# Values of a gated delta attention: four tap matmuls, or one projection convolved by GpSimd

## The chip, the cores and the metric

The kernel runs on one core of a Trainium2 chip. The core has a matrix engine (TensorE, PE), three engines for elementwise work (VectorE or DVE, ScalarE or ACT, GpSimd or POOL) and a queue that issues transfers (SyncE, SP). The metric is the device time of one launch in microseconds; lower is better. Every engine works through its own queue in order, and the queues meet at semaphores. GpSimd works on SBUF; matmul results lie in PSUM banks until VectorE or ScalarE takes them out.

## The reference

The program is four transformer layers with different attentions and feed-forward parts. The change is in the attention of the second layer, a gated delta rule over 4 sequences, run here on 1024 tokens each, with 8 heads of 128:

```python
mixed = einsum('bth,ch->btc', hidden_states, qkv_w)
mixed = causal_depthwise_conv(mixed, conv_w)      # 4 taps for each channel
z = einsum('bth,vh->btv', hidden_states, z_w)
q, k, v = split(mixed, 3)                         # 8 heads of 128 each
beta = sigmoid(bb); alpha = exp(-exp(A_log) * softplus(aa + dt_bias))
def step(S, inp):
    q_t, k_t, v_t, beta_t, alpha_t = inp
    S = S * alpha_t
    kv = einsum('bhk,bhkv->bhv', k_t, S)
    S = S + einsum('bhk,bhv->bhkv', k_t, (v_t - kv) * beta_t)
    return S, einsum('bhk,bhkv->bhv', q_t, S)
o = o * rsqrt(mean(o * o) + EPS) * norm_w * (z * sigmoid(z))
out = einsum('btv,hv->bth', o, out_w)
```

## The kernel before

The kernel solves the recurrence in chunks of 128 tokens. A chunk is one head and one block of 128 tokens in all four sequences at once, so most tiles are 128 x 4 x 128, written 128x512 in the profile. There are 8 heads x 8 blocks = 64 chunks (`CHUNKS`). The stage `a1s`, written by `delta_chunk_steps`, is one loop of 67 turns; every turn works on four chunks at different ages, which `phases(step)` names: `j` (the newest: keys and queries are projected and convolved, decay factors are made), `q` (the triangular system of the chunk is inverted), `r` (the state `S` is applied and updated), `e` (the output leaves). In the change "order" means the order of statements in this loop: each engine's queue is written out by hand.

What matters in a turn:

- The gram matrix of the keys (`gram_ps`, in `bank0`) times `Estrict` gives `N`; its diagonal blocks `Nc` are copied by ACT and masked by POOL into `lev`.
- The inverse is grown in six rounds. Round n: PE `zt(n)` (32 small matmul records from `lev` and `T`, L1035), ACT copies `Zt` (L1239), PE `tx(n)`, DVE `grow(n)` adds to `XTc` and transposes it into `T` (L1385, L1387). Round n+1 needs that `T`. Rounds 5 and 6 join blocks of 32 and of 64 in `XT`. PE puts other matmuls between `zt` and `tx` and between rounds.
- DVE's `place()` (L1391) copies four diagonal blocks of `XTc` into `XT` after round 4.
- Keys and queries are projected by one matmul each (L1143, L1161), copied into `hist` by ACT, and convolved by DVE: one tensor_scalar (L1371) and three scalar_tensor_tensor steps (L1373) for each of the two. These are the "conv" steps.
- The values are projected and convolved at once by PE. `xs` holds the chunk's normalized tokens with three tokens of history (copied by POOL, L1316, L1318), and the weights are held four times, scaled by each tap (ACT, L1215, once a head). `vtok_part(b)` adds up four matmuls of shifted tokens (L1109); ACT copies the result into `vtok`, which has tokens on the partitions.
- DVE multiplies `o` by the gate into `y` and, at the end of the turn, by the reciprocal of its root mean square (L1471); PE turns `y`, ACT copies `yT`, PE projects it out.
- POOL makes `newS`, `lev` (L1328, L1329), `sb` (L1335), `Estrict` (L1342) and `Eincl` (L1345).

The queue of PE for one turn is, in order: gram(q), kS(r), yT(e), qS(r), ktok(q), K raw(j), out(e), u(r), zt1, Q raw(j), tx1, o(r), zt2, S(r), tx2, dt(j), zt3, value part 0, tx3, part 1, zt4, part 2, tx4, part 3, zt5, qk(q), tx5, z(q), zt6, tx6. `Chain` is a helper that makes an engine wait for its own last instruction.

## Time and profile before

| | us |
|---|---|
| median of three runs | 8394.17 |
| lowest and highest | 8381.44 and 8395.7 |
| the profiled execution | 8398.92 |
| its span, first to last instruction | 8397.2 |

| engine | busy us in the span | share |
|---|---|---|
| PE | 7016.8 | 84% |
| DVE | 5867.6 | 70% |
| ACT | 4051.7 | 48% |
| POOL | 2918.4 | 35% |

The stage `a1s` runs from about 1041 to 2607 us of the span. "PE" rows are matmuls, "PEld" rows are weight loads, which overlap them. One float32 matmul leaves two records, so four matmuls read "x8". In a timeline row the first number is the start, the second the time from the first start to the last end of the merged instructions, and brackets hold the idle time of that engine before the row and what ended it. Group rows hold the count, then busy us and the mean ns of one, then idle time.

### The profile page before, as it was taken

How to read it: one execution, taken by the hardware profiler on the slowest of the kernel's cores; microseconds unless marked ns; L12 is line 12 of the kernel's file. 1: busy time of each engine (PE TensorE's matmuls, PEld its weight loads, DVE VectorE, ACT ScalarE, POOL GpSimd, SP SyncE). 2: the span in 40 equal slices, each digit the busy share in tenths (PEclk: the TensorE clock that was granted, in tenths of full speed). 3: DMA queues.
4: the chain of work that ended last, by engine and by line, in shares of the span. 5: the costliest groups of instructions: out<-in, count | busy, mean ns of one | idle time of the engine just before them, and what ended most of it. 6: DMA issues, size and time to landing. Idle time of an engine off the chain costs nothing. (4 is left out here: it accounts for less than half of the span.)

```text
span 8397.2 us, 277296 instructions
## 1 busy us (share of the span) xinstructions
PE 7016.8 (84%) x120944; PEld 4988.1 (59%) x120944; DVE 5867.6 (70%) x10703; ACT 4051.7 (48%) x6730; POOL 2918.4 (35%) x2152
## 2 busy tenths in 40 slices
PE   7999699999996997998997997998998779445566
PEld 3444478888885665665665665665665556345444
DVE  6665389999996885885885885885786657752366
ACT  3554145555553774774774775775775312210121
POOL 0101033333333773773773773773773000001000
PEclk8999599999998999998998998999999889555556
DMA  0000000000001221221221221221221000000000
GB/s 14 1 1 1 3 6 4 4 4 4 4 3 37 73 68 43 70 71 42 70 71 40 71 70 42 71 69 41 70 73 32 0 16 1 3 3 4 5 0 13
DMA packets 192003, 255.70 MB, mean 30 GB/s; under 512 B 59957, under 2 KB 86452, under 8 KB 189876
## 3 DMA queue, kind: packets, MB, share of 16 engines
q1 hardware_dynamic: 190772, 237.70, 10.7%
q8 instruction: 967, 15.84, 0.8%
q14 instruction: 264, 2.16, 0.1%
HBM read 27.84 MB, written 2.10 MB: 4 GB/s over the span
## 5 line engine op out<-in xcount | busy, mean ns | idle before, releaser
L1759 PE MATMUL wa_front<-w_wqkv,wa_xsT 128*128 128x512 f32 x2000 | 995.5, 621 | 39.5 <-PEq L66 20.4
L1681 POOL TENSOR_TENSOR XNT<-XNT 128x1024 f32<-128x1024 f32 x396 | 937.6, 2368 | 253.4 <-DVE XNT L1865 253.4
L1684 POOL TENSOR_TENSOR XNT<-XNT,wa_rnorm 128x1024 f32<-128x1024 f32 x330 | 627.9, 1903 | 364.5 <-DVE wa_rnorm L1873 364.5
L1862 DVE TENSOR_TENSOR XNT<-wa_front,w_scaled 128x1024 f32<-128x1024 f32 x330 | 393.6, 1193 | 309.9 <-ACT wa_sq L1700 228.0
L1759 PEld LDWEIGHTS wa_front<-w_wqkv,wa_xsT 128*128 128x128 f32 x2000 | 346.4, 193 | 317.7 <-issue 296.9
L446 PE MATMUL a0h_ring<-a0h_QT,a0h_KT 32*128 32x512 f32 (+3 forms) x1536 | 457.4, 567 | 14.2 <-ACT a0h_E L564 10.4
L564 ACT ACTIVATE a0h_E<-a0h_ring 128x512 f32<-128x512 f32 (+1 forms) x640 | 320.6, 554 | 296.7 <-PE a0h_ring L446 295.4
L1700 ACT ACTIVATE wa_sq<-wa_front 128x1024 f32<-128x1024 f32 x335 | 340.4, 1016 | 181.6 <-PE wa_front L1759 181.6
L1865 DVE TENSOR_TENSOR XNT<-wa_front,w_scaled 128x512 f32<-128x512 f32 x660 | 421.5, 680 | 0.0
L1878 DVE TENSOR_REDUCE wa_norm<-wa_sq 128x16 f32<-128x1024 f32 x330 | 399.0, 1209 | 0.0
L1765 PEld LDWEIGHTS wa_front<-consts,XNT 128*128 128x128 f32 x2640 | 297.7, 142 | 124.0 <-issue 56.7
L1765 PE MATMUL wa_front<-consts,XNT 128*128 128x128 f32 x2640 | 354.0, 277 | 14.2 <-POOL XNT L1684 9.6
L437 PE MATMUL a0h_slots<-a0h_KT,a0h_QT 32*128 32x512 f32 (+3 forms) x1536 | 349.2, 559 | 8.6 <-DVE a0h_part L643 3.4
L1903 DVE TENSOR_TENSOR wa_o<-wa_back,wa_rtotal 128x1024 f32<-128x1024 f32 x165 | 202.1, 1225 | 213.1 <-PE wa_back L1821 213.1
L606 POOL TENSOR_SCALAR_AFFINE_SELECT a0h_E<-a0h_E 128x512 f32<-128x512 f32 x128 | 79.7, 634 | 755.3 <-ACT a0h_E L564 755.3
L1847 PE MATMUL wa_back<-w_wo,wa_oT 128*128 128x128 f32 x2640 | 330.5, 280 | 5.6 <-ACT wa_oT L1745 5.6
L1342 POOL TENSOR_TENSOR a1s_Estrict<-a1s_E,a1s_sb 128x512 f32<-128x512 f32 x64 | 81.2, 1269 | 726.9 <-ACT a1s_E L1285 726.9
L1687 POOL TENSOR_TENSOR wa_sc<-wa_sc,wa_smax 128x1024 f32<-128x1024 f32 x160 | 304.4, 1902 | 68.9 <-DVE wa_smax L1916 68.9
L1847 PEld LDWEIGHTS wa_back<-w_wo,wa_oT 128*128 128x128 f32 x2640 | 315.6, 196 | 7.6 <-ACT wa_oT L1745 7.6
L1821 PEld LDWEIGHTS wa_back<-wa_v_look,wa_pT 64*32 64x32 f32 x21120 | 223.0, 106 | 156.2 <-issue 148.5
L643 DVE TENSOR_REDUCE a0h_part<-a0h_slots 128x2 f32<-128x1024 f32 (+3 forms) x256 | 257.2, 1021 | 78.6 <-PE a0h_slots L437 76.4
L1109 PE MATMUL a1s_bank<-a_w,a_xs 128*128 128x128 f32 x2048 | 297.5, 288 | 0.0
(636 smaller groups left out, 18302.9 us busy)
## 6 DMA issues: line engine op xcount, KB each, us to landing
wa_v_look<-wa_v_all SPq DMA_DIRECT2D x990, 128.0 KB, 2.4
wa_v_look<-wa_v_all SPq DMA_DIRECT2D x660, 64.0 KB, 2.0
wal_v_look<-wal_v_all SPq DMA_DIRECT2D x198, 128.0 KB
wal_v_look<-wal_v_all SPq DMA_DIRECT2D x132, 64.0 KB
w_wqkv<-in_L_ffn_Wqkv_dram SPq DMA_DIRECT2D x6, 1024.0 KB, 6.5
w_wo<-in_L_ffn_Wo_dram SPq DMA_DIRECT2D x6, 512.0 KB, 7.2
w_wqkv<-in_L_ffn_Wqkv_dram SPq DMA_DIRECT2D x12, 256.0 KB, 7.9
f2w_raw<-in_L_ffn_w_dram SPq DMA_DIRECT2D x48, 64.0 KB, 1.9
```

Of the source, the lines that this page charges most:

```text
L437: last = pe.matmul(o[:, i, at:at + w], QT[rows, n % 2, t * P:(t + 1) * P], KT[rows, n % 3, k * 512:k * 512 + w], start=True, stop=True)
L446: last = pe.matmul(o[:, at:at + w], KT[rows, n % 3, kb * P:(kb + 1) * P], QT2[rows, k, 512 - w:512], start=True, stop=True)
L564: a.activation(E[:, m % 3, j, 0:w], ring_of(key)[:, 0:w], ACT.Exp).then_inc(s["ring_a"], 1)
L1681: g.tensor_tensor(rot[:, at], rot[:, at], part[:, at], ALU.add).then_inc(s[summed], 1)
L1684: g.tensor_tensor(rot[:, at], rot[:, at], spread(rnorm[:, at, :], HDW), ALU.mult).then_inc(s[done], 1)
L1700: a.activation(sq[:, n].rearrange("p h d -> p (h d)"), two_banks(front, bank[n]), ACT.Square).then_inc(s[done], 1)
L1759: last = pe.matmul(front[:, first + i, :], xsT[:, slot, :], wqkv[:, (2 * n + i) * 512:(2 * n + i + 1) * 512], start=True, stop=True)
L1765: last = pe.transpose(front[:, first + i // 4, (i % 4) * P:(i % 4 + 1) * P], rot[:, n, 2 * i:2 * i + 2, :].rearrange("p h d -> p (h d)"), ...
L1847: last = pe.matmul(back[:, 0, 0:P], oT[:, i, :], wo[:, i, :], start=(i == 0), stop=(i == INNER // P - 1))
L1862: v.tensor_tensor(rot[:, n], src, cos, ALU.mult)
L1865: last = v.tensor_tensor(part[:, n, :, p0:p0 + 32], src[:, :, p1:p1 + 32], sin[:, :, p0:p0 + 32].broadcast_to([P, H, 32]), ALU.mult)
L1878: v.tensor_reduce(norm[:, n, :], sq[:, n], AX.X, ALU.add).then_inc(s[norm_in], 1)
```

## The change

The values are projected once (`project_v`, one 128x512 matmul into `bank6`), copied with three tokens of history into `vs` by ACT (`keep_v`), and convolved by POOL: four tensor_scalar multiplications into `parts`, two additions, into `vc`. PE transposes `vc` (`turn_v`), and ACT copies the result into `vtok` as before. The tap-scaled copies of the weights, `xs` and its copies are gone; projections read the normalized tokens directly. "Placing": the diagonal blocks of `XT` are placed by ACT, two in the middle of its turn and two at its end; round 5 reads `XTc`. "Scaling": `y` is scaled by ACT, and DVE makes only the reciprocal, earlier. "Order": gram and `N` of chunk `j` are made at the end of its own turn, between zt6 and tx6, so `Nc` follows there as well; POOL makes `lev` before `newS`, then the values. SP's loads of a head's weights and taps also wait for `v_ready` of the head before last. The core of the diff, with declarations, the `xs` to `xnt4` renamings and the removal of the ACT weight scaling left out:

```diff
                     elif n == 5:
-                        pe.wait_ge(s["x4_ready"], q + 1)
+                        pe.wait_ge(s["X_ready"], LD * q + 5)
                         hi = quarter(1)
                         for b in range(G):
...
                     else:
+                        pe.wait_ge(s["x4_ready"], 2 * q + 1)
                         pe.wait_ge(s["x5_ready"], q + 1)
...
-                def vtok_part(b):
+                def project_v():
+                    if j is None:
+                        return
+                    if r is not None:
+                        pe.wait_ge(s["s_used"], r + 1)
+                    pe.matmul(flat(bank[6][:]), weights(j)[:, V_W, :], xnt4[:, :, tokens(j)], start=True,
+                              stop=True).then_inc(s["vraw_ps"], 1)
+
+                def turn_v():
                     if q is None:
                         return
-                    if b == 0:
-                        pe.wait_ge(s["ktok_ready"], q + 1)
-                        if j is not None:
-                            pe.wait_ge(s["raw_copied"], 2 * j + 2)
-                    for n in range(TAPS):
-                        last = pe.matmul(bank[3][:, b, :], xs[:, q % 2, b, n:n + P], weights(q)[:, V_W + n, :], start=(n == 0),
-                                         stop=(n == TAPS - 1))
-                    if b == G - 1:
-                        last.then_inc(s["vtok_ps"], 1)
-
-                if q is not None:
-                    kq = conv[:, q % 3, K]
-                    pe.wait_ge(s["conv_ready"], 2 * q + 1)
-                    if q >= 1:
-                        pe.wait_ge(s["AT_ready"], q)
-                    pe.wait_ge(s["raw_copied"], 2 * q + 1)
-                    four_of(bank[0], lambda b: kq[:, b, :], lambda b: kq[:, b, :], s["gram_ps"])
+                    pe.wait_ge(s["ktok_ready"], q + 1)
+                    pe.wait_ge(s["v_ready"], q + 1)
+                    if j is not None:
+                        pe.wait_ge(s["raw_copied"], 2 * j + 2)
+                    turn_four(bank[3], vc, s["vtok_ps"])
...
                     pe.wait_ge(s["conv_ready"], 2 * r + 2)
+                    pe.wait_ge(s["vraw_copied"], min(step, CHUNKS))
                     four_of(bank[6], lambda b: conv[:, r % 3, QC, b, :], lambda b: S[:, b, :], s["qS_ps"])
...
                 zt(3)
-                vtok_part(0)
+                project_v()
                 tx(3)
-                vtok_part(1)
                 zt(4)
-                vtok_part(2)
+                turn_v()
                 tx(4)
-                vtok_part(3)
                 zt(5)
...
                 zt(6)
+                if j is not None:
+                    kq = conv[:, j % 3, K]
+                    pe.wait_ge(s["conv_ready"], 2 * j + 1)
+                    if j >= 1:
+                        pe.wait_ge(s["AT_ready"], j)
+                    pe.wait_ge(s["raw_copied"], 2 * j + 1)
+                    four_of(bank[0], lambda b: kq[:, b, :], lambda b: kq[:, b, :], s["gram_ps"])
                 if q is not None:
                     tx(6)
...
+                def keep_v():
+                    if j is None:
+                        return
+                    a.wait_ge(s["vraw_ps"], j + 1)
+                    if j >= 1:
+                        a.wait_ge(s["vs_kept"], j)
+                    a.activation(vs[:, :, T0:], bank[6][:], ACT.Copy).then_inc(s["vraw_copied"], 1)
+
+                def place(quarters):
+                    if q is None:
+                        return
+                    for k in quarters:
+                        last = a.activation(XT[quarter(k), q % 2, :, quarter(k)], XTc[quarter(k)], ACT.Copy)
+                    last.then_inc(s["x4_ready"], 1)
...
                     a.activation(T64[quarter(1), :, 0:32], bank[2][quarter(1), :, 0:32], ACT.Copy).then_inc(s["T64b_ready"], 1)
+                    if q >= 2:
+                        a.wait_ge(s["u_ps"], q - 1)
+                    place((2, 3))
                     a.wait_ge(s["z_ps"], q + 1)
                     a.activation(gatez[:, q % 2], bank[5][:], ACT.Tanh, scale=0.5).then_inc(s["tanh_ready"], 1)
                 evict_z(6)
+                keep_v()
+                if r is not None:
+                    a.wait_ge(s["gated"], r + 1)
+                    a.wait_ge(s["rstd_ready"], r + 1)
+                    for b in range(G):
+                        last = a.activation(y[:, b, :], y[:, b, :], ACT.Copy, scale=rstd[:, b:b + 1])
+                    last.then_inc(s["y_ready"], 1)
+                if j is not None:
+                    a.wait_ge(s["N_ready"], j + 1)
+                    if j >= 1:
+                        a.wait_ge(s["lev_ready"], j)
+                    for n in range(4):
+                        last = a.activation(Nc[quarter(n)], N[quarter(n), :, quarter(n)], ACT.Copy)
+                    last.then_inc(s["Nc_ready"], 1)
+                place((0, 1))
...
-                if j is not None:
-                    if j >= 2:
-                        g.wait_ge(s["z_ps"], j - 1)
-                        g.wait_ge(s["vtok_ps"], j - 1)
-                    at = j % BLOCKS * P
-                    if at == 0:
-                        g.memset(xs[:, j % 2, :, 0:T0], 0.0)
-                        g.tensor_copy(xs[:, j % 2, :, T0:], xnt4[:, :, 0:P]).then_inc(s["xs_ready"], 1)
-                    else:
-                        g.tensor_copy(xs[:, j % 2], xnt4[:, :, at - T0:at + P]).then_inc(s["xs_ready"], 1)
-                if r is not None:
-                    if r >= 1:
-                        g.wait_ge(s["s_used"], r)
-                    g.tensor_tensor(newS[:], S[:], spread(of_chunk(decays[:, 2], r), P), ALU.mult).then_inc(s["newS_ready"], 1)
                 if q is not None:
                     g.wait_ge(s["Nc_ready"], q + 1)
                     if q >= 1:
@@ -1329,6 +1344,26 @@
                     g.tensor_tensor(lev[:, 1:SMALL], Nc[:].unsqueeze(1).broadcast_to([P, SMALL - 1, G, 32]),
                                     small[:, 1:SMALL, :].unsqueeze(2).broadcast_to([P, SMALL - 1, G, 32]),
                                     ALU.mult).then_inc(s["lev_ready"], 1)
+                if r is not None:
+                    if r >= 1:
+                        g.wait_ge(s["s_used"], r)
+                    g.tensor_tensor(newS[:], S[:], spread(of_chunk(decays[:, 2], r), P), ALU.mult).then_inc(s["newS_ready"], 1)
+                if q is not None:
+                    t = taps[:, q // BLOCKS % 2, 2]
+                    g.wait_ge(s["vraw_copied"], q + 1)
+                    if q >= 1:
+                        g.wait_ge(s["vtok_ps"], q)
+                    for i in range(TAPS):
+                        last = g.tensor_scalar(parts[:, i], vs[:, :, i:i + P], t[:, i:i + 1], None, ALU.mult)
+                    chain(last)
+                    chain(g.tensor_tensor(parts[:, 0:2], parts[:, 0:2], parts[:, 2:4], ALU.add))
+                    g.tensor_tensor(vc[:], parts[:, 0], parts[:, 1], ALU.add).then_inc(s["v_ready"], 1)
+                    g.wait_ge(s["v_ready"], q + 1)
+                    if q < CHUNKS - 1:
+                        if q % BLOCKS < BLOCKS - 1:
+                            g.tensor_copy(vs[:, :, 0:T0], vs[:, :, P:P + T0]).then_inc(s["vs_kept"], 1)
+                        else:
+                            g.memset(vs[:, :, 0:T0], 0.0).then_inc(s["vs_kept"], 1)
...
-                def place():
-                    for k in range(4):
-                        last = v.tensor_copy(XT[quarter(k), slot, :, quarter(k)], XTc[quarter(k)])
-                    last.then_inc(s["x4_ready"], 1)
-
-                if q is not None:
-                    v.wait_ge(s["gram_ps"], q + 1)
-                    v.wait_ge(s["strict_ready"], q + 1)
-                    v.tensor_tensor(N[:], bank[0][:], Estrict[:], ALU.mult).then_inc(s["N_ready"], 1)
...
+                    if q >= 1:
+                        v.wait_ge(s["x4_ready"], 2 * q)
                     v.tensor_tensor(XTc[:], lev[:, 0], ident, ALU.add).then_inc(s["X_ready"], 1)
...
-                    v.tensor_tensor(y[:], o[:], gatez[:, r % 2], ALU.mult)
+                    v.tensor_tensor(y[:], o[:], gatez[:, r % 2], ALU.mult).then_inc(s["gated"], 1)
                 grow(3)
                 convolve(1, 0, 2)
                 grow(4)
-                if q is not None:
-                    place()
+                if r is not None:
+                    v.wait_ge(s["std_ready"], r + 1)
+                    v.reciprocal(rstd[:], std[:]).then_inc(s["rstd_ready"], 1)
...
+                if j is not None:
+                    v.wait_ge(s["gram_ps"], j + 1)
+                    v.wait_ge(s["strict_ready"], j + 1)
+                    v.tensor_tensor(N[:], bank[0][:], Estrict[:], ALU.mult).then_inc(s["N_ready"], 1)
+                if q is not None:
                     v.wait_ge(s["x_ps"], LX * q + 6)
                     v.tensor_copy(XT[0:64, slot, :, 64:P], bank[4][0:64, :, 0:64]).then_inc(s["x6_ready"], 1)
-                if r is not None:
-                    v.wait_ge(s["std_ready"], r + 1)
-                    chain(v.reciprocal(rstd[:], std[:]))
-                    v.tensor_tensor(y[:], y[:], spread(rstd[:], P), ALU.mult).then_inc(s["y_ready"], 1)
             v.wait_ge(s["added"], CHUNKS)
```

## Rows read from the trace of the kernel before

**Rows 1.** Windows, busy us of each engine (count), then granted clock, DMA share, GB/s.

```profile
1200.00:1600.00 400.00, 381.79 (x7234) 324.59 (x7232) 361.27 (x669) 203.15 (x533) 124.41 (x137) 1.00 0.02 4
```

**Rows 2.** One line's instructions, all of the span: ns min/median/max, first and last start.

```profile
L1342 POOL TENSOR_TENSOR a1s_Estrict<-a1s_E,a1s_sb x64: 1263/1266/1463, 1056.3 to 2561.6; 128x512 f32<-128x512 f32 x64
```

**Rows 3.** Groups of instructions by form, in the delta stage.

```profile
L1109 PE MATMUL a1s_bank<-a_w,a_xs 128*128 128x128 f32 x2048 | 297.5, 288 | 0.0
...
L1391 DVE COPY a_XT<-a1s_XTc 32x128 f32<-32x128 f32 x256 | 119.7, 468 | 2.6
...
L1471 DVE TENSOR_TENSOR a1s_y<-a1s_y,a1s_rstd 128x512 f32<-128x512 f32 x63 | 94.9, 1506 | 2.2
```

**Rows 4.** Timeline of PE, one turn.

```profile
1984.23 1.16 PE L1109 MATMUL a1s_bank<-a_w,a_xs 128*128 128x128 f32 x8
1985.32 0.45 PE L1035 MATMUL a1s_bank<-a1s_T,a1s_lev 32*32 32x32 f32 x32
...
1990.08 0.31 PE L1087 MATMUL a1s_bank<-a1s_Zt,a_XT 32*32 32x32 f32 x5 [0.28 <-DVE a_XT L1391]
...
1990.57 1.16 PE L1022 MATMUL a1s_bank<-a_w,a_xs 128*128 128x128 f32 x8
...
1992.82 0.68 PE L1097 MATMUL a1s_bank<-a_XT,a1s_Zt 64*64 64x64 f32 x8 [0.48 <-ACT a1s_Zt L1241]
...
1994.42 1.06 PE L1022 MATMUL a1s_bank<-a_S,a1s_conv 128*128 128x128 f32 x8
...
1996.98 0.60 PE L1027 MATMUL a1s_bank<-consts,a1s_conv 128*128 128x128 f32 x4
1997.42 1.02 PE L1143 MATMUL a1s_bank<-a_xs,a_w 128*128 128x512 f32 x2
...
2000.25 0.45 PE L1035 MATMUL a1s_bank<-a1s_T,a1s_lev 32*32 32x32 f32 x32
```

**Rows 5.** Timeline of DVE, the same turn.

```profile
1998.42 1.34 DVE L1411 TENSOR_TENSOR a1s_XTc<-a1s_lev,a_small 128x128 f32<-128x128 f32 x1 [0.35 <-POOL a1s_lev L1328]
...
2000.03 0.65 DVE L1420 TENSOR_TENSOR X<-a1s_bank,X 128x512 f32<-128x512 f32 x1
2000.61 0.68 DVE L1423 TENSOR_TENSOR a1s_u<-a1s_bank,a_beta_all 128x512 f32<-128x512 f32 x1
...
2008.87 0.45 DVE L1371 TENSOR_SCALAR a1s_conv<-a_hist,a_taps 128x512 f32<-128x512 f32 x1
```

**Rows 6.** Timeline of ACT, the turn before it.

```profile
1985.85 0.28 ACT L1239 ACTIVATE a1s_Zt<-a1s_bank 128x128 f32<-128x128 f32 x1 [1.05 <-PE a1s_bank L1035]
...
1988.37 0.60 ACT L1288 ACTIVATE a1s_vtok<-a1s_bank 128x512 f32<-128x512 f32 x1 [0.33 <-PE a1s_bank L1109]
...
1989.50 0.28 ACT L1239 ACTIVATE a1s_Zt<-a1s_bank 128x128 f32<-128x128 f32 x1
```

**Rows 7.** Timeline of POOL, the turn of rows 5.

```profile
1998.34 1.27 POOL L1329 TENSOR_TENSOR a1s_lev<-a1s_Nc,a_small 128x512 f32<-128x512 f32 x1
```

**Rows 8.** Timeline of DVE at the start of the stage.

```profile
1053.13 0.49 DVE L1371 TENSOR_SCALAR a1s_conv<-a_hist,a_taps 128x512 f32<-128x512 f32 x1 [10.83 <-ACT a_hist L1249]
1053.66 2.33 DVE L1373 SCALAR_TENSOR_TENSOR a1s_conv<-a_hist,a_taps,a1s_conv 128x512 f32<-128x512 f32 x3
...
1056.42 4.17 DVE L1373 SCALAR_TENSOR_TENSOR a1s_conv<-a_hist,a_taps,a1s_conv 128x512 f32<-128x512 f32 x3
```

**Rows 9.** Timeline of POOL at the start of the stage.

```profile
1057.54 1.71 POOL L1345 TENSOR_TENSOR a1s_Eincl<-a1s_E,consts 128x512 f32<-128x512 f32 x1
```

**Rows 10.** Groups of POOL over the whole span.

```profile
L1681 POOL TENSOR_TENSOR XNT<-XNT 128x1024 f32<-128x1024 f32 x396 | 937.6, 2368 | 253.4 <-DVE XNT L1865 253.4
...
L606 POOL TENSOR_SCALAR_AFFINE_SELECT a0h_E<-a0h_E 128x512 f32<-128x512 f32 x128 | 79.7, 634 | 755.3 <-ACT a0h_E L564 755.3
...
L1322 POOL TENSOR_TENSOR a1s_newS<-a_S,a_decays 128x512 f32<-128x512 f32 x64 | 67.4, 1052 | 6.0 <-DVE a_S L1439 6.0
```

**Rows 11.** Windows, 5 us at the end of the stage.

```profile
2590.00:2595.00 5.00, 4.77 (x29) 4.58 (x28) 2.27 (x5) 0.60 (x1) 0.00 (x0) 0.66 0.00 0
```

More of the change, by code:

```diff
@@ L932, in l1_attention_stage @@
         with Stage(nc, "a1s") as st:
-            delta_chunk_steps(nc, st, X, xnt4, c, d, w, raw_w, taps, half_norm, S, hist, g_all, beta_all, nb_all, XT, T64, xs,
+            delta_chunk_steps(nc, st, X, xnt4, c, d, w, raw_w, taps, half_norm, S, hist, g_all, beta_all, nb_all, XT, T64, vs,
                               eps, small, decays)
@@ L942, in quarter, with delta_chunk_steps @@
     return slice(32 * n, 32 * n + 32)
-def delta_chunk_steps(nc, st, X, xnt4, c, d, w, raw_w, taps, half_norm, S, hist, g_all, beta_all, nb_all, XT, T64, xs, eps,
+def delta_chunk_steps(nc, st, X, xnt4, c, d, w, raw_w, taps, half_norm, S, hist, g_all, beta_all, nb_all, XT, T64, vs, eps,
                       small, decays):
@@ L963, in delta_chunk_steps @@
                 "gatez_ready qk_ps AT_ready kS_ps qS_ps qS_used R_ready u_ps u_ready uend_ready o_ps o_done s_ps "
-                "loaded scaled w_ps w_ready newS_ready s_used msq_ready std_ready y_ready yT_ps yT_ready out_ps added chain")
+                "loaded w_ps vraw_ps vraw_copied vs_kept v_chain v_ready w_ready newS_ready s_used msq_ready std_ready gated rstd_ready y_ready yT_ps yT_ready out_ps added chain")
     K, T0 = 0, TAPS - 1
@@ L993, in _ @@
                     sp.wait_ge(s["conv_ready"], 2 * BLOCKS * (n - 1))
+                    sp.wait_ge(s["v_ready"], BLOCKS * (n - 1))
                 for k in range(3):
@@ L1012, in turn_weights @@
                     pe.wait_ge(s["w_ready"], 2 * n + 1)
-                    pe.wait_ge(s["scaled"], n + 1)
                     if n >= 1:
                         pe.wait_ge(s["T64b_ready"], step)
-                for k, m in enumerate((0, 1, 3, 4) if part == 0 else (2, 5, 6, 7)):
+                for k, m in enumerate((0, 1, 3, 4) if part == 0 else (2,)):
                     last = pe.transpose(bank[2][:, k, :], raw_w[:, m, :], c.ident)
@@ L1083, in tx @@
                     elif n == 5:
-                        pe.wait_ge(s["x4_ready"], q + 1)
+                        pe.wait_ge(s["X_ready"], LD * q + 5)
                         hi = quarter(1)
                         for b in range(G):
-                            last = pe.matmul(bank[2][hi, b, 0:32], XT[hi, v, b, hi], Zt[hi, b, :], start=True, stop=True)
+                            last = pe.matmul(bank[2][hi, b, 0:32], XTc[hi, b, :], Zt[hi, b, :], start=True, stop=True)
                         last.then_inc(s["t_ps"], 1)
@@ L1091, in tx @@
                                 last = pe.matmul(bank[4][quarter(lo), b, 0:32], Zt[quarter(hi), b, :],
-                                                 XT[quarter(hi), v, b, quarter(hi)], start=True, stop=True)
+                                                 XTc[quarter(hi), b, :], start=True, stop=True)
                         last.then_inc(s["x_ps"], 1)
                     else:
+                        pe.wait_ge(s["x4_ready"], 2 * q + 1)
                         pe.wait_ge(s["x5_ready"], q + 1)
@@ L1142, in _ @@
                         pe.wait_ge(s["N_ready"], q + 1)
-                    pe.matmul(flat(bank[0][:]), weights(j)[:, K_W, :], xs[:, j % 2, :, T0:], start=True,
+                    pe.matmul(flat(bank[0][:]), weights(j)[:, K_W, :], xnt4[:, :, tokens(j)], start=True,
                               stop=True).then_inc(s["raw_ps"], 1)
@@ L1160, in _ @@
                         pe.wait_ge(s["ktok_ready"], q + 1)
-                    pe.matmul(flat(bank[3][:]), weights(j)[:, Q_W, :], xs[:, j % 2, :, T0:], start=True,
+                    pe.matmul(flat(bank[3][:]), weights(j)[:, Q_W, :], xnt4[:, :, tokens(j)], start=True,
                               stop=True).then_inc(s["raw_ps"], 1)
@@ L1196, in _ @@
                         pe.wait_ge(s["o_done"], r + 1)
-                    four_of(bank[5], lambda b: xs[:, q % 2, b, T0:], lambda b: weights(q)[:, Z_W, :], s["z_ps"])
+                    four_of(bank[5], lambda b: xnt4[:, b, tokens(q)], lambda b: weights(q)[:, Z_W, :], s["z_ps"])
                 zt(6)
+                if j is not None:
[5 more added lines that the diff above has]
+                    four_of(bank[0], lambda b: kq[:, b, :], lambda b: kq[:, b, :], s["gram_ps"])
                 if q is not None:
@@ L1209, in keep_weights @@
                 into = w[:, n % 2]
-                if part == 0:
-                    a.wait_ge(s["loaded"], 8 * 16 * (n + 1))
-                    if n >= 1:
-                        a.wait_ge(s["w_ps"], 2 * n)
-                    for i in reversed(range(TAPS)):
-                        last = a.activation(raw_w[:, 2 if i == 0 else 4 + i, :], raw_w[:, 2, :], ACT.Copy,
-                                            scale=taps[:, n % 2, 2, i:i + 1])
-                    last.then_inc(s["scaled"], 1)
                 a.wait_ge(s["w_ps"], 2 * n + 1 + part)
@@ L1224, in keep_weights @@
                 else:
-                    a.activation(into[:, V_W:V_W + TAPS, :], bank[2][:], ACT.Copy).then_inc(s["w_ready"], 1)
+                    a.activation(into[:, V_W, :], bank[2][:, 0, :], ACT.Copy).then_inc(s["w_ready"], 1)
             keep_weights(0, 0)
@@ L1249, in keep_raw @@
                     a.activation(hist[:, n, :, T0:], bank[at][:], ACT.Copy).then_inc(s["raw_copied"], 1)
-                if q is not None:
-                    a.wait_ge(s["N_ready"], q + 1)
-                    if q >= 1:
-                        a.wait_ge(s["lev_ready"], q)
-                    for n in range(4):
-                        last = a.activation(Nc[quarter(n)], N[quarter(n), :, quarter(n)], ACT.Copy)
-                    last.then_inc(s["Nc_ready"], 1)
                 if e is not None:
```

17 lines of the change are left out of this document (11 added, 6 removed).

## The prediction

> **What bounds the kernel now.** I read the page first: its 40 slices show one stretch in which TensorE (PE) stays at 9 tenths, and the windows of that stretch say why it matters: in 400 us of the delta stage PE is busy 382, VectorE (DVE) 361, ScalarE (ACT) 203, GpSimd (POOL) 124, at a granted clock of 1.00 [rows 1]. The stage is 67 turns of one loop; the 64 POOL products `Estrict` start between 1056.3 and 2561.6 [rows 2], so a turn takes 1505.3/63 = 23.9 us. Next I read PE's timeline of one turn. It is one unbroken queue but for two short waits, 0.28 before tx(5) and 0.48 before tx(6) [rows 4]: PE is the bound, with 0.8 us of slack in a turn. DVE is at 90%, so the second limit is close. The third thing to see is not in any busy share: what DVE and POOL do to each other. `XTc<-lev,small`, 128x128, took 1.34 us on DVE after POOL had begun `lev` 0.08 us before it, and `X<-bank,X`, four times as large, took 0.65 beside another POOL product [rows 5, 7]. At the stage's start, three `conv` steps that ran alone took 2.33 us; the next three, which met POOL's `Estrict` and `Eincl`, took 4.17, and POOL's `Eincl` took 1.71 [rows 8, 9] where the median of the same-sized `Estrict` is 1.27 [rows 2]. So a DVE instruction that reads two SBUF tensors and a POOL instruction that reads SBUF exclude each other: whichever comes second waits for the whole of the other. DVE instructions that take one operand from PSUM pass freely.
>
> The Trainium skill says the same (page "SBUF — State Buffer", section "Who interferes with whom": the pair of ports is an exclusive lock, for DVE operations with two SBUF inputs or in a 2-port mode). By that rule the work that this change gives to POOL costs DVE time wherever the two meet; by a reading of the busy shares alone it would be free. The trace sides with the rule.
>
> **The change, part by part.**
>
> PE. The 16 value matmuls of a turn go: each four takes 1.09 (1984.23 to 1985.32) [rows 4], so 4.36; over the stage they are the costliest PE group, 297.5 us in x2048 records [rows 3]. Added are one projection, 128x512, for which `K raw` gives 1.02, and four transposes at 0.44 (1996.98 to 1997.42) [rows 4]: 1.46. PE's own work falls by 2.9, from 23.1 to 20.2 us. If PE alone set the time this would be 64 x 2.9 = 186 us.
>
> But those matmuls lay in four pieces between zt and tx and covered the chain PE -> ACT (`Zt`) -> PE -> DVE (`XTc`, `T`) -> PE. I therefore follow the loop that ties one turn to the next after the change, in three legs.
>
> Leg A, PE in order, tx(5) to the end of `u` in the next turn: tx(5) 0.49, z 1.09 (like a value group of four), zt(6) 0.60 (like tx(6)); tx(6) and one group of four 1.60 (1992.82 to 1994.42: `gram` now stands before tx(6) and fills the 0.48 wait); then from kS to zt(1) 5.83 (1994.42 to 2000.25) [rows 4]. With 0.1 to DVE's start: 9.7 us.
>
> Leg B, DVE from `u` to the third `T`: 2000.61 to 2008.87, 8.26 [rows 5], less about 0.2 that it stood waiting for tx(3), so 8.1.
>
> Leg C, zt(4), `Zt`, then ACT's own queue: `Zt` at 1985.85 to the end of the fifth `Zt` at 1989.78 is 3.93, with the table load, `E`, `vtok`, `T64` in between; less 0.33, a wait for the value matmuls [rows 6]; with 0.6 for zt(4) and releases and 0.1 to tx(5): 4.3. The shorter PE queue does not shorten this leg.
>
> Sum 9.7 + 8.1 + 4.3 = 22.1 us a turn without port stalls. So of the 2.9 saved, 1.8 would show.
>
> DVE. `place` (four copies, mean 0.468) and the scaling of `y` (1.51) go [rows 3]: 3.4 us, part of it blocking by POOL, since the scaling took 1.51 where `X<-bank,X` of that size takes 0.65. They lay behind the third `T`, partly under leg C, so in the sum they buy little. ACT gains `place` (4 x 0.3), four scaled copies of `y` (about 1.3) and one eviction (0.6): some 3.1 us on 12.1, put where ACT waited. `y`, then `Nc`, are ready at about 0.8 and 2.0 us after kS starts; kS leaves room for `yT` until 1.1, and zt(1) is due at 5.8. I cost them at nothing; without that cover every us late at `y` is a us. The head's weights lose three transposes and five ACT operations, under 2 us in each of 7 turns, nothing beside the rest. SP's added wait on `v_ready` holds loads that are used four turns later: nothing.
>
> POOL. It loses `xs` and gains four 128x512 scalings, an addition of 128x1024, one of 128x512 and a small copy. No row shows a POOL tensor_scalar; below it is the one-input select of that size, 0.63, above a two-input product, 1.05 (`newS`) [rows 10]. I take 0.6, as it has one tensor to read. The wide addition is `XNT<-XNT`, 2.37 [rows 10], the other 1.27 [rows 2]. POOL's list from `Nc` on, about 2.0 us after kS: lev0 0.4 (an estimate, a quarter of `lev`), lev 1.2, newS 1.0, scalings 2.4, 2.3, 1.2, copy 0.2, `sb` 1.0 like newS: 9.7 us without a gap. Before, it had lev0, lev and `sb` in that place and then rested until `E` came. The value is needed by the transposes at about 15; it is in time.
>
> What hides all this is that POOL rests. It now doesn't, and leg B passes in front of it. Times from kS: lev ends at 4.7 and lets DVE's first `XTc` through by 5.0, `T` and `X` end at 5.9, just when `u` is due. `uend` asks at 6.6, in the second scaling: 0.5 lost. `o`, XTc+T pass freely. The third and fourth scaling end at 9.0, the wide addition asks at 9.15, while DVE's `conv` scaling (0.45, 0.49 with its start [rows 8]) holds the port until 9.43; the addition follows, the next `conv` step asks at 9.5 and waits for it until 11.8: 2.3 lost. `o`, `S`, XTc+T pass, the next two `conv` steps meet `sb`: 0.8 lost. Sum 3.6 us in leg B. The last `conv` step of the turn comes just before `Estrict` and loses nothing. PE stands idle at zt(3) meanwhile.
>
> A turn: 22.1 + 3.6 = 25.7 against 23.9, or +1.8; 64 turns make +115 us. The profiled execution took 8398.9 us (span 8397.2), the median is 8394.2, 0.06% less: 8509, rounded 8510.
>
> Bounds of the stall. Above: from `u` on POOL has 1.8 + 2.3 + 1.2 + 0.2 + 1.1 = 6.6 us of work, some 2.9 run beside the DVE steps that read PSUM, so 3.7; with 1.05 for a scaling 1.8 more, so 5.5, or 8630. Below: the instants above are uncertain by some tenths. If newS ends 0.1 later, `uend` passes, `conv`'s first step meets the fourth scaling (0.55), the two later ones the tails of the two additions (0.4, 1.2) and the product with the gate meets `sb` (1.1): 3.4. If the first step passes free, 2.8: 8460. With none lost it is 8280.
>
> **The rivals.**
> *The port costs little*, the one on the other side. Six DVE instructions of leg B need the port; the timing of both queues may settle so that POOL waits for DVE, as `Eincl` did. For it: POOL has some 4 us of spare time before its value is due. Against: even with POOL at 31% of a turn, DVE lost about 1.1 of the 1.34 us of `XTc` in every one. It decides when less than 1.8 us are lost per turn. Time: 8280 with none, about 8340 with 1 us. Chance 0.25.
> *Even*: 1.5 to 2.1 us lost, 8375 to 8413. Chance 0.08.
> *PE is still the bound* and all 2.9 show: 8210. It needs zt(4) and zt(5) right behind tx(3) and tx(4), though the `T` between takes 0.45 + 0.6 us. Chance 0.02, counted as faster.
> *The clock falls.* PE's idle time rises from 0.8 to 5.5 us a turn (25.7 less 20.2); when PE thinned out at the end of the stage the granted clock of 5 us was 0.66 [rows 11], part of it at 1.2 GHz. If a quarter of the stage's PE work ran so: 64 x 20.2 / 4 = +320, 8830. Against: PE's gaps are 2 us at most. Chance 0.05, slower.
> *Forecast*, 2.4 to 5.5 us lost: 8430 to 8630. Chance 0.60.
>
> **How the numbers follow.** A measurement of this kernel can tell about 0.2%, 17 us, from no change. Slower 0.60 + 0.05 = 0.65, same 0.08, faster 0.27. The range reaches up to the bound, 8630, and down to 8320, into the rival on the other side, leaving 0.1 above and 0.1 below. The forecast's own range is 8430 to 8630.
>
> **What would show it.** The period of `Estrict` near 25.7; `conv` steps (0.75 alone) with some near 3 us and `uend` above 0.69; DVE idle small from `u` to the third `T`; PE waiting some 2 us at zt(3) for `T`; no wait of PE for `v_ready`; no block before `y`'s transposes. If the mean `conv` step stays under 0.9, the port term is wrong. If the period is about 22, leg sums hold and stalls do not; if POOL's scaling takes over 1 us, the upper bound applies.

## The result, and the profile after

The changed kernel takes 8724.17 us (median of 4 runs, 8712.29 to 8747.07), beside it the kernel before 8390.29: ratio 1.0402 [1.0379, 1.0426], so 4.0% or 334 us slower. The forecast was slower, 8510, with a range up to 8630; the direction holds, the size doesn't, and the time lies above the range. I look first where the time was added, then inside one turn.

The span and mean clock of the core, the windows of [rows 1] and two kinds of group, all of the kernel after. The columns of the window are those of [rows 1], the third figure from the end of the line being the granted clock as a share of 2.4 GHz:

```profile
core 0: 8724.2 us, clock 0.846
```

```profile
1200.00:1600.00 400.00, 339.54 (x5493) 282.21 (x5494) 298.95 (x475) 205.86 (x548) 245.53 (x189) 0.78 0.02 4
```

One line's instructions of the kernel after (ns min/median/max, first and last start):

```profile
L1377 POOL TENSOR_TENSOR a1s_Estrict<-a1s_E,a1s_sb x64: 1262/1265/1640, 1039.0 to 2877.2; 128x512 f32<-128x512 f32 x64
L1357 POOL TENSOR_SCALAR a1s_parts<-a_vs,a_taps x256: 1553/1562/2527, 1046.9 to 2895.3; 128x512 f32<-128x512 f32 x128
L1360 POOL TENSOR_TENSOR a1s_vc<-a1s_parts x64: 1588/1593/1602, 1055.9 to 2899.4; 128x512 f32<-128x512 f32 x64
```

Groups of the kernel after in the delta stage (busy us, mean ns of one):

```profile
L1359 POOL TENSOR_TENSOR a1s_parts<-a1s_parts 128x1024 f32<-128x1024 f32 x64 | 158.3, 2474 | 5.3
...
L1408 DVE SCALAR_TENSOR_TENSOR a1s_conv<-a_hist,a_taps,a1s_conv 128x512 f32<-128x512 f32 x384 | 459.2, 1196 | 9.1
```

`Estrict` starts 64 times between 1039.0 and 2877.2: a turn takes 1838.2/63 = 29.2 us against 23.9 [rows 2], and 5.3 x 64 = 339 us is the whole difference. So nothing outside the turns matters. POOL went from 124 to 246 us of each 400, as meant. But PE fell from 382 to 340 [rows 1], and DVE from 361 to 299: neither engine is full any more, and the granted clock is 0.78 where it was 1.00. At full clock PE's 20.2 us of work in 29.2 would be 277 us of 400; it was busy 340, since part of that work took twice its time.

Windows of 3 and 5 us through one turn of the kernel after show which part:

```profile
2003.00:2006.00 3.00, 3.00 (x35) 2.71 (x35) 1.12 (x4) 0.88 (x3) 0.00 (x0) 0.50 0.00 0
2006.00:2009.00 3.00, 3.00 (x17) 2.66 (x17) 1.06 (x2) 1.47 (x3) 1.41 (x2) 0.50 0.01 3
2009.00:2012.00 3.00, 3.00 (x18) 2.66 (x17) 1.11 (x2) 2.52 (x9) 0.00 (x0) 0.50 0.00 0
2012.00:2015.00 3.00, 3.00 (x21) 3.00 (x20) 1.81 (x2) 1.31 (x4) 2.82 (x4) 0.68 0.00 0
2015.00:2020.00 5.00, 5.00 (x89) 3.56 (x88) 4.59 (x9) 2.03 (x4) 5.00 (x3) 1.00 0.02 3
2020.00:2025.00 5.00, 4.68 (x121) 3.95 (x121) 4.86 (x10) 1.91 (x12) 4.91 (x3) 1.00 0.01 3
2025.00:2030.00 5.00, 2.46 (x102) 1.44 (x100) 4.86 (x8) 2.58 (x4) 3.59 (x3) 1.00 0.00 0
2030.00:2033.00 3.00, 1.69 (x21) 1.63 (x22) 2.93 (x5) 2.38 (x6) 1.26 (x1) 0.66 0.03 8
2033.00:2036.00 3.00, 3.00 (x35) 2.71 (x35) 1.18 (x4) 0.88 (x3) 0.00 (x0) 0.50 0.00 0
```

From 2003 to 2012 PE never rests and runs at 0.50, that is 1.2 GHz; from 2015 to 2030 it runs at 1.00, 2.4 GHz. Ahead of the fall it was busy only 2.46 of 5 us. Two windows of 1 us place the fall: the clock is 0.98 from 2030 to 2031, while PE stands still, and 0.50 from 2031 on, before its next matmul at 2031.31:

```profile
2030.00:2031.00 1.00, 0.00 (x0) 0.00 (x0) 0.93 (x3) 0.99 (x2) 0.00 (x0) 0.98 0.10 25
2031.00:2032.00 1.00, 0.69 (x17) 0.63 (x17) 1.00 (x3) 0.99 (x4) 0.78 (x1) 0.50 0.00 0
```

It is so in all turns: from 1200 to 2400 us the granted clock is 0.79, which is 29.2 x 0.21 x 2 = 12 us of each turn at the half clock, and none of the 63 turns is free of it. PE's timeline of the turn names both the gaps and the price:

```profile
2002.14 2.08 PE L1028 MATMUL a1s_bank<-a1s_conv 128*128 128x128 f32 x8
2004.14 0.47 PE L1093 MATMUL a1s_bank<-a1s_Zt,a1s_XTc 32*32 32x32 f32 x5
...
2004.95 2.08 PE L1028 MATMUL a1s_bank<-a_w,XNT 128*128 128x128 f32 x8
2006.96 1.11 PE L1071 MATMUL a1s_bank<-a_T,a1s_N 64*64 64x64 f32 x8
2008.00 2.07 PE L1028 MATMUL a1s_bank<-a1s_conv 128*128 128x128 f32 x8
...
2011.05 2.07 PE L1028 MATMUL a1s_bank<-a_S,a1s_conv 128*128 128x128 f32 x8
...
2016.91 1.06 PE L1028 MATMUL a1s_bank<-a1s_R,a_XT 128*128 128x128 f32 x8
...
2028.42 0.45 PE L1041 MATMUL a1s_bank<-a1s_T,a1s_lev 32*32 32x32 f32 x32 [2.38 <-DVE a1s_T L1422]
...
2031.31 0.64 PE L1063 MATMUL a1s_bank<-a1s_T,a1s_N 32*32 32x32 f32 x16 [1.47 <-DVE a1s_T L1422]
...
2033.88 0.47 PE L1093 MATMUL a1s_bank<-a1s_Zt,a1s_XTc 32*32 32x32 f32 x5
```

Four groups of four 128x128 matmuls stand here with 2.07 or 2.08 us; the same group at 2016.91 takes 1.06. Two waits for DVE's `T`, 2.38 before zt(4) and 1.47 before zt(5), stand at the end of the fast stretch, and the clock falls within the second. PE's waits from 1200 to 2400 us (total, times, longest), some 41 turns, show that this turn is no exception; the first line holds the waits before zt(3) and zt(4), the second those before zt(5):

```profile
PE a1s_bank L1041 <- DVE a1s_T L1422: 127.9, 68, 3.7
PE a1s_bank L1063 <- DVE a1s_T L1422: 47.8, 41, 2.3
```

What DVE did meanwhile, and POOL beside it, in the same turn:

```profile
2018.73 0.69 DVE L1453 TENSOR_TENSOR a1s_uend<-a1s_u,a_decays 128x512 f32<-128x512 f32 x1
...
2021.17 1.05 DVE L1408 SCALAR_TENSOR_TENSOR a1s_conv<-a_hist,a_taps,a1s_conv 128x512 f32<-128x512 f32 x1
...
2024.02 3.20 DVE L1408 SCALAR_TENSOR_TENSOR a1s_conv<-a_hist,a_taps,a1s_conv 128x512 f32<-128x512 f32 x2
...
2028.29 0.72 DVE L1406 TENSOR_SCALAR a1s_conv<-a_hist,a_taps 128x512 f32<-128x512 f32 x1
```

```profile
2014.84 7.72 POOL L1357 TENSOR_SCALAR a1s_parts<-a_vs,a_taps 128x512 f32<-128x512 f32 x4
2022.64 2.35 POOL L1359 TENSOR_TENSOR a1s_parts<-a1s_parts 128x1024 f32<-128x1024 f32 x1
2025.07 1.60 POOL L1360 TENSOR_TENSOR a1s_vc<-a1s_parts 128x512 f32<-128x512 f32 x1
2026.73 0.54 POOL L1364 COPY a_vs<-a_vs 128x12 f32<-128x12 f32 x1
2027.23 1.49 POOL L1370 TENSOR_TENSOR a1s_sb<-consts,a_nb_all 128x512 f32<-128x512 f32 x1
```

POOL works without a gap from 2012.2 to 2028.7. Two `conv` steps, asked at 2024.02 beside the wide addition, take 3.20 together; alone two take 1.5. The `T` behind them is late, and PE waits 2.38.

The legs of the prediction can be read in the same trace. Means over 57 turns, from the starts of tx(5) and `u` and the end of the third `T`: A 12.8, B 10.8, C 5.7 us. The forecast had 9.7, 11.7 (8.1 with 3.6 of stalls) and 4.3. Leg B is shorter than forecast. All that is missing lies in A and C. The prediction gave C to ACT, but at the half clock PE sets it: qk takes 2.08 from 2002.14, and tx(5) follows it at 2004.14, though ACT's fifth `Zt` was there at 2002.64:

```profile
2002.36 0.28 ACT L1241 ACTIVATE a1s_Zt<-a1s_bank 128x128 f32<-128x128 f32 x1
```

### The profile page after: what moved, and what is told of

The parts are those of the page before. It is cut to its first block and busy times, and to the rows that moved or that the text cites. A ratio compares the mean times of both kernels' runs of the same rounds, so it can differ in the third digit from the quotient of the medians.

```text
span 8724.2 us, 274760 instructions
## 1 busy us (share of the span) xinstructions
PE 7124.0 (82%) x119256; PEld 5051.1 (58%) x119256; DVE 5913.7 (68%) x10384; ACT 4236.9 (49%) x7274; POOL 3627.9 (42%) x2527
## 5 line engine op out<-in xcount | busy, mean ns | idle before, releaser
L1408 DVE SCALAR_TENSOR_TENSOR a1s_conv<-a_hist,a_taps,a1s_conv 128x512 f32<-128x512 f32 x384 | 459.2, 1196 | 9.1
L1357 POOL TENSOR_SCALAR a1s_parts<-a_vs,a_taps 128x512 f32<-128x512 f32 x256 | 445.6, 1755 | 0.0
```

Source lines behind the costliest of these rows:

```text
L1357: last = g.tensor_scalar(parts[:, i], vs[:, :, i:i + P], t[:, i:i + 1], None, ALU.mult)
L1408: last = v.scalar_tensor_tensor(out=into, in0=hist[:, n, :, i:i + P], scalar=t[:, i:i + 1], in1=into, op0=ALU.mult, op1=ALU.add)
```

## The experiments

Two theories. *Clock*: DVE's stalls open gaps on PE, the clock falls to 1.2 GHz for some 10 us of each turn, and that makes up what the forecast lacks. *Port*: POOL's list holds DVE up far more than 3.6 us, and the low clock is a mere companion. Ratios are those to the kernel before, run on the same chip; turns are worked out from `Estrict` as in [rows 2].

**e1_warm: the changed kernel with ten idle matmuls.** They write a bank that is free then, and nobody reads them.

```
+ def fill(n):                          # skipped when q is None
+     pe.wait_ge(s["o_done"], r + 1)    # when r is not None
+     for b in range(n):
+         pe.matmul(bank[5][:, b % G, :], c.ones, c.upto, start=True, stop=True)
  tx(3)
+ fill(6)
  zt(4)
  turn_v()
  tx(4)
+ fill(4)
  zt(5)
```

> The changed kernel plus ten idle matmuls a turn (128x128, constants, into a bank that is free then): six before PE's wait at zt(4), four before its wait at zt(5), 2.7 us of PE work. Results are unchanged. Clock theory: in the changed kernel the granted clock of the stage is 0.78 and PE runs qk to yT, ten us of each turn, at half speed because it idled 2.4 and 1.5 us just before; with the gaps filled the clock is above 0.95, the turn falls from 29.2 to about 24.5 us, and the kernel takes 8430 us (8400 to 8480). Port theory: DVE's waits for POOL alone make the turn long, PE's speed is off the path; the clock comes back and the time stays within 50 us of 8724, or rises by up to 64 x 2.7 = 170 us.

Measured 8567.8, 1.0221 [1.0204, 1.0238]; turn 26.7, granted clock 0.94 from 1200 to 2400. More work on PE took 156 us off the time. That is for *clock*, but less than expected (8400 to 8480): the clock still fell for a part of 50 of the 63 turns. The 13 that kept the full clock throughout take 25.8 us on average (24.4 to 26.9).

**e2_noconv: without POOL's convolution.** Its four scalings and two additions become one copy.

```
- for i in range(TAPS):
-     last = g.tensor_scalar(parts[:, i], vs[:, :, i:i + P], t[:, i:i + 1], None, ALU.mult)
- chain(last)
- chain(g.tensor_tensor(parts[:, 0:2], parts[:, 0:2], parts[:, 2:4], ALU.add))
- g.tensor_tensor(vc[:], parts[:, 0], parts[:, 1], ALU.add).then_inc(s["v_ready"], 1)
+ g.tensor_copy(vc[:], vs[:, :, T0:]).then_inc(s["v_ready"], 1)
```

> The changed kernel with POOL's six convolution instructions replaced by one copy of the projected values: the values are not convolved. POOL's list shrinks by some 9.5 us a turn. The leg sum of the prediction says 22.1 us a turn without port stalls, so 8280 us, with the clock near 1.00. Rival: the chain through zt(4) and zt(5) has lost its cover even without POOL, PE idles there and its clock falls: turn above 25 us, 8460 us or more.

Measured 8444.6, 1.0085 [1.0058, 1.0112]; turn 24.8, clock 0.88. This lies between the two forecasts. The `conv` step is back at 744 ns, so its port stalls are gone, and yet the kernel is slower than before. Of its 63 turns, 20 take about 22 us, 23 take 26.8 to 28.3 and the others lie between: with the stalls away the clock still fell in many of them. The 11 turns without any half clock average 22.2 us, the 22.1 of the leg sum. The two theories are not exclusive; the next runs separate their shares.

**e6_noconv_warm: both edits at once**, e2 with e1's matmuls.

> The changed kernel without POOL's convolution (one copy in its place, the values are not convolved) and with the ten idle matmuls of e1. Both causes gone: the leg sum of 22.1 us a turn at a clock of 1.00, 8280 us (8270 to 8310). In e2 single turns had 21.7 to 22.3 but their mean was 24.8. If instead the mean stays above 23.5, something else than clock and port makes e2's long turns.

**e10_warm18: e1 with more idle matmuls**, 12 and 6 in place of 6 and 4, sent later to hold the clock in every turn.

> e1 with eighteen idle matmuls (twelve before zt(4), six before zt(5)) in place of ten. POOL's whole list stays. In e1 the clock was 0.94 and the turn 26.7 us. Clock theory: at a clock of 0.99 or more the turn shows the port alone. With e6 (22.9 us, no list) the difference is what the list costs; I expect 25.7 us a turn, as the prediction's walk had it, 8510 us. Rival: the extra idle matmuls only delay PE where it did not wait: no gain on e1 or slower, above 8560.

e6 took 8333.6, 0.9924 [0.9907, 0.9940], turn 22.9, above the 8270 to 8310 expected. e10 took 8498.9, 1.0136 [1.0120, 1.0151], turn 25.8, as the clock theory expected. The windows from 1200 to 2400 us of e6, then of e10 (columns as in [rows 1]):

```profile
1200.00:2400.00 1200.00, 1184.52 (x22573) 977.54 (x22572) 981.17 (x1838) 782.53 (x2114) 444.39 (x473) 1.00 0.02 4
```

```profile
1200.00:2400.00 1200.00, 1139.97 (x20777) 952.69 (x20777) 1069.86 (x1633) 699.90 (x1885) 870.49 (x654) 1.00 0.02 4
```

Both have the full clock, so what is left between them is POOL's list: 25.8 - 22.9 = 2.9 us a turn. That is the least it costs, for in e6 PE is busy 1184.52 of 1200 us, full again with the 2.7 us of idle matmuls on top of its 20.2; against the full-clock turns of e2, which has none, the list costs 25.8 - 22.2 = 3.6. The eight more idle matmuls of e10 don't show: the full-clock turns of e1, with ten, are as long.

The difference between the changed kernel and e10 is the price of the clock, at least 29.2 - 25.8 = 3.4 us a turn, 225.3 us by the medians, though e10 has 18 matmuls more on PE. DVE's hold-ups are not what changed between the two. By mean times, the instructions that POOL holds up (six `conv` steps, two `conv` scalings, `R`, `uend` and `y`) take 6 x 1.20 + 2 x 0.67 + 1.19 + 0.76 + 1.19 = 11.7 us a turn in the changed kernel and 6 x 1.16 + 2 x 0.72 + 0.72 + 0.78 + 1.94 = 11.8 in e10. DVE's groups of e10, then of e6, say where the list cost time:

```profile
L1418 DVE SCALAR_TENSOR_TENSOR a1s_conv<-a_hist,a_taps,a1s_conv 128x512 f32<-128x512 f32 x383 | 442.6, 1156 | 9.1
L1485 DVE TENSOR_TENSOR a1s_y<-a1s_o,a1s_gatez 128x512 f32<-128x512 f32 x64 | 124.3, 1942 | 0.0
```

```profile
L1414 DVE SCALAR_TENSOR_TENSOR a1s_conv<-a_hist,a_taps,a1s_conv 128x512 f32<-128x512 f32 x384 | 286.0, 745 | 9.1
...
L1481 DVE TENSOR_TENSOR a1s_y<-a1s_o,a1s_gatez 128x512 f32<-128x512 f32 x64 | 44.3, 693 | 0.0
```

Six `conv` steps at 0.41 more and `y` at 1.25 more are 3.7 us of DVE's time in a turn, and the two `conv` scalings at 0.28 more (0.72 against 0.45) another 0.6; 2.9 to 3.6 of it reaches the turn.

**e5_before_pool: the list alone, on the kernel before.** POOL's six instructions run on a buffer of zeros, with nothing else of the change; nobody uses their result.

```
+ for i in range(TAPS):
+     last = g.tensor_scalar(parts[:, i], vs[:, :, i:i + P], nb_all[:, i, 0:1], None, ALU.mult)
+ chain(last)
+ chain(g.tensor_tensor(parts[:, 0:2], parts[:, 0:2], parts[:, 2:4], ALU.add))
+ chain(g.tensor_tensor(vc[:], parts[:, 0], parts[:, 1], ALU.add))
```

> The kernel before, unchanged but for POOL, which after lev also runs the six convolution instructions on a tile of zeros; nothing reads their result. PE keeps all its work and its cover. Port theory: DVE, at 90% before, loses some 3 to 5 us a turn to POOL and becomes the bound: 26 to 28 us a turn, 8530 to 8650 us, with PE's clock somewhat below 1.00 for it now waits. Rival: the four value groups between zt and tx absorb the delay: under 24.3 us a turn, under 8420.

Measured 8818.4, 1.0507 [1.0485, 1.0528], turn 30.7, clock 0.83: far above the 8530 to 8650 expected, and a larger loss than the whole change. PE has its full 23.1 us of work here, and still it waits for `T`, and still the clock falls. From the waits of e5, 1200 to 2400 us (total, times, longest; the same wait of the kernel before came to 1.7 us in 6):

```profile
PE a1s_bank L1036 <- DVE a1s_T L1396: 135.7, 69, 3.3
```

So POOL's list by itself causes the waits and with them the low clock; the thinner PE queue is not needed for it.

**e4_pe_values: all the rest of the change**, placing, scaling of `y` and order as after, the values by TensorE as before.

```
- zt(3); project_v(); tx(3); zt(4); turn_v(); tx(4)
+ zt(3); vtok_part(0); tx(3); vtok_part(1); zt(4); vtok_part(2); tx(4); vtok_part(3)
- g.tensor_scalar(...) x4, g.tensor_tensor(...) x2, g.tensor_copy(vs...)
+ g.tensor_copy(xs[:, j % 2], xnt4[:, :, at - T0:at + P])
```

> Placing, scaling and order as in the changed kernel, but the values projected and convolved by PE with tap-scaled weights as before; POOL has no convolution. PE stays the bound with its waits gone: 23.1 to 23.4 us a turn, clock 1.00, 8340 to 8370 us, a little faster than before. Rival: y, Nc and the blocks of XT now come late from ACT and PE waits for them: slower than before, over 8400.

Measured 8351.9, 0.9963 [0.9947, 0.9978], turn 23.4, clock 1.00. This is as expected. Those parts gain 0.4%, and all the loss is the values' move.

**e3_tt: the scalings as products**, with the taps as a broadcast second tensor in place of `tensor_scalar`.

```
- last = g.tensor_scalar(parts[:, i], vs[:, :, i:i + P], t[:, i:i + 1], None, ALU.mult)
+ last = g.tensor_tensor(parts[:, i], vs[:, :, i:i + P],
+                        t[:, i:i + 1].unsqueeze(2).broadcast_to(four), ALU.mult)
```

> The changed kernel with POOL's four tensor_scalar (1.56 us each when undisturbed) written as products of two tensors with the taps broadcast (1.05 us each expected, as newS). Results are unchanged. Price theory: the length of POOL's list makes the stalls, 2 us less a turn, so the kernel gains 60 to 130 us on 8724. Hold theory: DVE is held only during the first 0.5 us of POOL's tensor_scalar but during all of a product, so DVE loses as much or more: within 30 us of 8724 or slower.

Measured 8762.9, 1.0458 [1.0437, 1.0478]. The product takes 1.09 us (median) where `tensor_scalar` takes 1.56, so POOL has some 2 us less to do; the kernel is 39 us slower all the same. `uend`, 0.76 us after, takes 0.90 here. Less time on POOL is not less time of DVE at the port: the same sum as above is 11.3 us a turn here against 11.7, so of the 2 us only 0.4 reach DVE. As the clock stays low (0.78), the run does not weigh the port by itself.

**e7_act_scales: the four scalings on ScalarE**, in two pairs where it waits for PE; POOL keeps the two additions. **e8_act_scales_warm** adds the idle matmuls (6 and 4), **e11_act_scales_warm6** only 3 and 3.

```
+ def scale_v(half):
+     for i in (0, 1) if half == 0 else (2, 3):
+         last = a.activation(parts[:, i], vs[:, :, i:i + P], ACT.Copy,
+                             scale=taps[:, q // BLOCKS % 2, 2, i:i + 1])
+     last.then_inc(s["scaled_v"], 1)
  keep_raw(0, 0)
+ scale_v(0)
  evict_z(1)
  keep_raw(1, 3)
+ scale_v(1)
  evict_z(2)
```

> The changed kernel with the four tap scalings done by ACT (0.6 us each, placed before its first two waits for Zt) and only the two additions left to POOL. Results are unchanged. POOL's list is 6.2 us shorter, but DVE was held only about 0.5 us by each scaling. Both theories give a gain: 26 to 27 us a turn with the clock still low in part, 8520 to 8590. Rival: ACT's queue, 2.4 us longer, delays Zt and hist: no gain on 8724.

> e7 with the ten idle matmuls of e1. Results are unchanged. Port stalls of about 2.5 us remain: 24.3 us a turn at a clock above 0.97, 8420 us (8370 to 8460). If the port was only a small part of e1's 26.7 us, it stays near 8560.

> e8 with six idle matmuls (three and three) in place of ten. In e8 the clock was 1.00 and PE waited 0.4 us at each of the two places. If 1.1 us less idle work still keeps the clock, the turn falls by up to 0.5 us: 8335 us. If not, single turns of 28 us return and the time is above 8420.

Measured: e7 8625.0, 1.0266 [1.0249, 1.0283], turn 27.5, clock 0.80; e8 8364.6, 0.9967 [0.9955, 0.9980], turn 23.5, clock 1.00; e11 8374.4, 0.9986 [0.9977, 0.9996]. Taking 6.2 us of scalings off POOL gains 1.7 us a turn without the matmuls; ten idle matmuls then gain 4.0 more. e7 gained less than expected (8520 to 8590), e8 more (8370 to 8460), and e11 met neither of its forecasts. e10 to e8, both at full clock, puts the scalings at 2.2 us a turn. More than half of what DVE gets back is `y`, 1.94 in e10 and 0.78 in e8, so the scalings cost mainly by pushing the additions later, under `y`. e8 to e6 leaves 0.7 for the two additions, again the least, as e6 is full on PE. Fewer idle matmuls (e11) are not better than more.

**e9_pair_sums: a version made from all this.** ScalarE scales, POOL makes one 128x1024 addition into pairs, and PE sums the two of a pair while it turns them. Those eight matmuls are real work in the place of the idle ones.

```
- chain(g.tensor_tensor(parts[:, 0:2], parts[:, 0:2], parts[:, 2:4], ALU.add))
- g.tensor_tensor(vc[:], parts[:, 0], parts[:, 1], ALU.add).then_inc(s["v_ready"], 1)
+ g.tensor_tensor(pairs[:, q % 2], parts[:, 0:2], parts[:, 2:4], ALU.add).then_inc(s["v_ready"], 1)
- turn_v()            # four transposes, after zt(4)
+ turn_v(0); turn_v(1); zt(4); turn_v(2); tx(4); turn_v(3); zt(5)
+     # in turn_v(b): for n in range(2): pe.matmul(bank[3][:, b, :], pairs[:, q % 2, n, b, :],
+     #                                            c.ident, start=(n == 0), stop=(n == 1))
```

> From e7: ACT scales the four taps, POOL makes one addition of 128x1024 (two pair sums), and PE adds the two while it turns them: eight matmuls with the identity (2.2 us) instead of four transposes (0.45) in the places where the value groups stood, no idle matmuls. Results are unchanged. POOL's list is 7.8 us shorter than in the changed kernel, PE's work 1.7 us longer and spread where it waited. If the clock holds: 22.9 to 23.3 us a turn, 8330 to 8360 us, below before and level with e4 or e8. Rival: PE still waits over 1 us at zt(4) for DVE, the clock falls: above 8450.

Measured 8337.3, 0.9948 [0.9934, 0.9961], turn 23.1, as expected. Windows of e9, and PE's longest waits (total, times, longest):

```profile
1200.00:2400.00 1200.00, 1131.73 (x21908) 927.02 (x21907) 1019.61 (x1820) 907.38 (x2304) 560.09 (x467) 1.00 0.02 4
```

```profile
PE a1s_bank L1041 <- DVE a1s_T L1436: 32.0, 53, 0.8
PE a1s_bank L1063 <- DVE a1s_T L1436: 25.7, 52, 0.5
```

It beats both kernels, by 0.5% and 4.4%; beside e4 (0.9963 [0.9947, 0.9978]) it is no different by their intervals.

## Why the prediction was wrong in size

**What bounds the kernel: right.** PE was the bound with DVE close behind, and what the change did to DVE decided.

**The PE sum and the three legs: right as a sum.** At full clock the legs of e10 are A 9.7, B 11.1, C 4.9 (means over 57 turns) against 9.7, 11.7 and 4.3. The forecast turn was 25.7, e10's is 25.8; the forecast time 8510, e10's 8499. That it comes so near is in part luck, since B and C miss by 0.6 us each, in opposite directions. With the list away, e6 has B at 8.4 against 8.1; its turn of 22.9 is PE's own work with the idle matmuls, and the full-clock turns of e2 take 22.2 against the forecast 22.1.

**The port stalls: the sum near, its parts not.** 3.6 was forecast; e10 gives 2.9 against e6 and 3.6 against the full-clock turns of e2. Two errors nearly cancelled, which is luck. POOL's `tensor_scalar` was taken at 0.6 us from [rows 10]; it takes 1.56 alone. By the upper bound of the prediction (1.8 more for a scaling of 1.05) this should have cost well over 5 us. But it doesn't hold DVE for its whole time: `uend` asks in the midst of the four scalings and takes 0.69 (2018.73 above), its time alone; the last section has 40 such cases. The rule that whichever comes second waits for the whole of the other was too wide there. `conv` steps did meet the wide addition and `sb`, as forecast (24 and 22 times in e10 from 1200 to 2400 us). New are the `conv` scalings and `y`, which in the same stretch began during an addition 36 times (only the prediction's lower case had it held up at all); `uend` lost 0.07 us (0.76 against 0.69) where 0.5 was forecast. The forecast also had PE wait some 2 us at zt(3). It waits 0.8 there on average, 2.3 at zt(4) and 1.2 at zt(5) (57 turns): the four scalings took 7.72 us where 2.4 was put, so the additions came a round later, and the two longest gaps came side by side. Last, the prediction's lower case adds up to 3.25, not 3.4; that is 10 us of time, and nothing rests on it.

**The step that failed** is the rival *The clock falls*, at a chance of 0.05 on the argument "PE's gaps are 2 us at most". So the clock's term in the sum was put at nothing. The trace has 2.38 and 1.47 us, three microseconds apart, in the turn shown, waits of up to 3.7 us elsewhere, and some of every turn at the half clock. I had PE's idle time in a turn about right (5.5 us forecast, (1200 - 1019.39) / 41.1 = 4.4 measured) and had [rows 11] to show 0.66, but judged by the length of one gap. The two gaps stand close together, where zt(4) and zt(5) each wait for one `T` behind a held `conv` step. The work that follows, some 10 us of it here, then runs at 1.2 GHz: qk, tx(5), z, zt(6), `gram`, tx(6), kS, all of it leg A and the end of leg C. The rival's price, a quarter of PE's work at half rate, was 320 us by itself and 8830 in all. Measured: 3.4 us a turn, 225 us, and 8724. With this term in its place the sum is 25.7 + 3.4 = 29.1 a turn against 29.2 measured; the 3.4 itself is a measurement, and no row of the kernel before gives it.

The Trainium skill (page "TensorE: Matmul & The Clock Gate", section "HAM oscillation — how this bites in real kernels") describes a loop in which a wait in each pass makes the clock fall, so that every pass begins at the half clock. The windows of one turn above agree on the loop: 0.50 at 2003, 1.00 at 2015, 0.50 again at 2033. The waits of the page's loop are longer than the 2.38 and 1.47 us here, so the page does not by itself say that these two would do it; the trace does. The rival deserved more than 0.05 all the same, since the loop gives the clock a chance to fall in each of 64 turns. That it falls in one does not mean that it falls in all, as e1 and e2 show.

**Costed at nothing, and so:** `place` and the scaling of `y` on ACT, the head's weights, SP's wait: e4 has all but the last two and is faster by 0.4%; no run separates those two. **What would have shown it:** I named the mean `conv` step; it is 1.20, above the 0.9 that would have spoken against the port term. I named no check of the granted clock by windows inside a turn, which shows the fault at one look.

**Left open.** What decides whether the clock falls in a given turn isn't settled: in e2 PE's longest wait was 1.2 us and it fell in many turns; in e10 the longest was 0.9, in e9 0.8, and it didn't; but in e8 the longest was 1.1 and in e11 1.7, and the granted clock stayed at 1.00 and 0.99. So the longest wait alone does not tell them apart. Why POOL's `tensor_scalar` is slower than a product is open too.

## What to carry to other kernels

When a change thins out the engine that sets the time, put its idle time on a line, turn by turn, and ask what the granted clock does at the two longest gaps: 4.4 us of waiting in a turn went with 12 us at the half clock here. Moving work from TensorE to GpSimd is not free for VectorE; price each GpSimd instruction by how long it holds VectorE's second input, and give what can be done from one input to ScalarE. If a chain on another engine must leave gaps on TensorE, spread real matmuls over them, or even idle ones, as the turns of 25.8 us with 18 idle ones against 29.2 without show.
